# Attention scores in groups of four tiles over four PSUM banks, one PSUM bank for all transpositions, and an order of work drawn anew

## The reference

```
h = x @ W ; e = leaky_relu(h@a0 + (h@a1)^T) masked by adj ; alpha = softmax(e)
x = layernorm(x + concat(alpha @ h, h))                       # layer 0, 256 features
q, k, v = x@Wq.T+bq, x@Wk.T+bk, x@Wv.T+bv                     # layer 1, 8 heads of 64
attn = softmax(mask(q k^T / 8)) ; y = (attn @ v) @ Wo.T + bo
x = layernorm(x + y)
```

## Time and profile before

| | |
|---|---|
| time, median of 3 runs | 3236.22 us (3234.52 to 3239.79) |
| the profiled execution | 3235.14 us, of which its span is 3233.3 us |
| PE busy | 3015.4 us (93%) |
| DVE busy | 2604.6 us (81%) |
| ACT busy | 2427.2 us (75%) |
| POOL busy | 2070.5 us (64%) |
| share of the DMA engines, main queue | 73.8% |
| granted TensorE clock, mean | 0.988 |

### The profile page before, as it was taken

One profiled execution on the slowest core, in us unless ns is written; L12 is line 12 of the kernel. 1 busy time (PEld: TensorE's weight loads), 2 busy tenths in 40 slices (PEclk: granted clock), 3 DMA queues, 4 the chain that ended last, 5 costly groups with the idle time before them and its releaser, 6 DMA issues.

```text
span 3233.3 us, 60175 instructions
## 1 busy us (share of the span) xinstructions
PE 3015.4 (93%) x19084; PEld 2496.1 (77%) x19084; DVE 2604.6 (81%) x6553; ACT 2427.2 (75%) x5383; POOL 2070.5 (64%) x1799
## 2 busy tenths in 40 slices
PE   5899999999999999999999999999999999999995
PEld 4787788777787787787777787777887777887874
DVE  4888888888888888888888888888888888888873
ACT  4777777777777777877777877777877778777764
POOL 1566676666666666766666666666666666766664
PEclk8999999999999999999999999999999999999997
DMA  3777777777777777787777777777777777777774
GB/s 124 201 207 213 223 214 226 208 209 215 217 222 221 207 212 214 222 230 213 208 210 222 221 224 212 210 210 217 222 224 208 205 214 222 220 227 206 212 203 143
DMA packets 290044, 681.90 MB, mean 211 GB/s; under 512 B 40512, under 2 KB 74048, under 8 KB 256960
## 3 DMA queue, kind: packets, MB, share of 16 engines
q1 hardware_dynamic: 289728, 678.05, 73.8%
HBM read 375.40 MB, written 302.51 MB: 210 GB/s over the span
## 4 chain that ended last, share of the span: by engine, by line
PE 49%; DMA 25%; POOL 10%; SPq 5%; ACT 5%; issue 3%; DVE 3%; ACTq 0%; DVEq 0%; POOLq 0%
PE R_bank L621 30%; DMA turned_lo_prob<-scratch 17%; PE O_bank L708 9%; POOL turned_lo_prob L1054 8%; DMA scratch<-blocked 8%; PE S_bank L689 6%; SPq L523 4%; PE L_bank L612 2%; ACT turned_hi_prob L736 2%; DVE blocked L995 1%; SPq L540 1%; POOL turned L1074 1%; PE L_bank L621 1%; POOL o_pair L1049 1%; DVE prob L975 1%
## 5 line engine op out<-in xcount | busy, mean ns | idle before, releaser
L1054 POOL TENSOR_TENSOR turned_lo_prob<-turned_lo_prob,turned_hi_prob 128x512 fp32r<-128x512 f32 x1024 | 1312.0, 1312 | 671.5 <-ACT turned_hi_prob L736 671.5
L995 DVE STREAM_TRANSPOSE blocked<-prob 128x512 f32<-128x512 f32 x1024 | 695.4, 699 | 185.9 <-ACT prob L817 127.9
L736 ACT ACTIVATE turned_hi_prob<-turned_lo_prob 128x512 fp32r<-128x512 f32 x1024 | 593.5, 622 | 329.1 <-DMA turned_lo_prob<-scratch 322.8
L817 ACT ACTIVATE prob<-prob,negmax 128x512 f32<-128x512 f32 x1024 | 730.3, 714 | 89.2 <-DVE negmax L975 88.1
L975 DVE CUSTOM_DVE_ANT_0 prob<-S_bank,mask 128x512 f32<-128x512 f32 x1024 | 681.1, 679 | 83.5 <-PE S_bank L689 77.1
L689 PE MATMUL S_bank<-qk_pair 64*128 64x512 f32 x3072 | 495.3, 427 | 84.9 <-DVE negmax L975 83.5
L708 PE MATMUL O_bank<-turned_hi_prob,v_st 128*128 128x256 f32 x2048 | 517.6, 290 | 48.9 <-POOL turned_lo_prob L1054 48.5
L708 PE MATMUL O_bank<-turned_lo_prob,v_st 128*128 128x256 f32 x2048 | 508.4, 285 | 0.0
L708 PEld LDWEIGHTS O_bank<-turned_hi_prob,v_st 128*128 128x128 f32 x2048 | 396.6, 194 | 73.2 <-POOL turned_lo_prob L1054 67.9
L621 PE MATMUL R_bank<-wv,x1T 128*128 128x256 f32 x3072 | 415.4, 288 | 0.2 <-DVE v_st L874 0.2
L621 PEld LDWEIGHTS R_bank<-wv,x1T 128*128 128x128 f32 x3072 | 381.7, 191 | 38.3 <-issue 35.5
(11 more groups left out here) (75 smaller groups left out, 4315.6 us busy)
## 6 DMA issues: line engine op xcount, KB each, us to landing
scratch<-blocked SPq DMA_DIRECT2D x256, 1024.0 KB, 4.6
turned_lo_prob<-scratch SPq DMA_DIRECT2D x1024, 256.0 KB, 5.6
tokens<-xT SPq DMA_DIRECT2D x128, 256.0 KB, 5.0
tokens<-x SPq DMA_DIRECT2D x128, 256.0 KB, 4.8
r_wide<-r_scratch SPq DMA_DIRECT2D x512, 64.0 KB, 3.6
out<-tokens SPq DMA_DIRECT2D x128, 256.0 KB, 4.0
r_scratch<-r_cols SPq DMA_DIRECT2D x256, 2.0 KB
tokens<-adj SPq DMA_DIRECT2D x1, 1024.0 KB, 7.6
```

Of the source, the lines that this page charges most:

```text
L736: act.activation(dst, src, ACT.Copy).then_inc(done, 1)
L817: act.activation(prob_tile(R, s), prob_tile(R, s), ACT.Exp, bias=negmax[:, slot:slot + 1], scale=-1.0, accum_out=psum_row[:, ph % 2, j:j + ...
L995: dve.transpose(blocked[:, ph % 2, :, :, 2 * (s % 2) + s % 4 // 2, :].rearrange("p d c i -> p c d i"), prob_tile(R, s).rearrange("p (c d i ...
L1054: pool.tensor_tensor(turned_lo_prob[:, ph % 2, a, :, :], turned_lo_prob[:, ph % 2, a, :, :].bitcast(F32), turned_hi_prob[:, a, :, :].bitca ...
```

## The change

1. `scores` becomes a group of two units, four tiles, in four banks. `S_bank` has 4 banks instead of 3, tile s stands in bank s % 4, and a group waits until all four tiles of the group before it are reduced. There are 8 groups in a round where there were 16 units.
2. `L_bank` is one bank instead of two. Every solo piece waits until the one before it is taken out.
3. `N` is copied to SBUF by ACT (`n_wide`, one copy of 128x512 a round), and `pre` reads it from there. So the bank is free at once.
4. `pair` becomes `turn`: the weighted sums go to `oT` a half at a time (8 a round of 128x256 on ACT and on POOL, where there were 4 of 128x512), and the buffer `o_half` holds one half, where `o_pair` held two. `lows` of a half waits for the low part of the half before it.
5. The small buffers are packed together, and `stats` gets 2 rows instead of 4.
6. All five tables, the start, the prologue and the ending are written in a new order.

```diff
-        S_bank = [bank(f"S_bank{i}") for i in range(3)]
+        S_bank = [bank(f"S_bank{i}") for i in range(4)]
-        L_bank = [bank(f"L_bank{i}") for i in range(2)]
+        L_bank = bank("L_bank")
...
-            return S_bank[(32 * R.k + s) % 3]
+            return S_bank[s % 4]
...
-                before = solo_count(R, name, 1 - SAME_BANK.get(name, 2))
+                before = solo_count(R, name, 0)
...
-            def scores(R, u):
-                pair, t = u // T, u % T
+            def scores(R, g):
+                pair = g // 2
...
-                if t == 0:
+                if g % 2 == 0:
                     pe.wait_ge(ring_done, R.ring(f"k{pair}", 1))
-                if due(R.n(32, 2 * u - 1)):
-                    pe.wait_ge(s_red, R.n(32, 2 * u - 1))
-                for j, (qp, kp) in enumerate(PARTS):
-                    for w in range(2):
+                if due(R.n(32, 4 * g)):
+                    pe.wait_ge(s_red, R.n(32, 4 * g))
+                for u in (2 * g, 2 * g + 1):
+                    t = u % T
+                    for j, (qp, kp) in enumerate(PARTS):
+                        for w in range(2):
...
                 if kind == "pre":
                     if i == 0:
-                        act.wait_ge(n_mm, R.nx(1, 1))
+                        act.wait_ge(n_copied, R.nx(1, 1))
...
-                    act.activation(alpha[:, :], L_bank[0][:, :], ACT.Prelu, bias=terms[:, i, 0:1],
+                    act.activation(alpha[:, :], n_wide[:, :], ACT.Prelu, bias=terms[:, i, 0:1],
                                    alpha=LEAK).then_inc(a_pre, 1)
+                if kind == "N":
+                    act.wait_ge(n_mm, R.nx(1, 1))
+                    act.activation(n_wide[:, :], L_bank[:, :], ACT.Copy).then_inc(n_copied, 1)
...
-                if u % 2 == 0 and due(R.n(4, u // 2)):
-                    act.wait_ge(o_lo, R.n(4, u // 2))
+                if due(R.n(8, u)):
+                    act.wait_ge(o_lo, R.n(8, u))
...
-            def pair_hi(R, pair):
-                if pair == 0 and R.last:
+            def half_hi(R, u):
+                if u == 0 and R.last:
                     act.wait_ge(ring_mm, R.ring("O3", 1))
-                act.wait_ge(o_normed, R.n(8, 2 * pair + 2))
-                split_hi(oT[:, HI, pair % 4, :], o_pair[:, :], o_hi)
+                act.wait_ge(o_normed, R.n(8, u + 1))
+                split_hi(oT[:, HI, u // 2 % 4, o_cols(u % 2)], o_half[:, :], o_hi)
```

One line of the tables, of TensorE's near the middle of a round:

```diff
-    "E1 scores scores",
-    "V0 A3 V1",
+    "scores E1",
+    "V0 E2",
```

More of the change, by code:

```diff
@@ L77 @@
-    "B3",
+    "N k1",
+    "weigh weigh",
+    "A3 C0",
+    "scores O0",
+    "O1 O2",
+    "scores weigh",
+    "weigh O3",
+    "q2 k2",
+    "C1 D0",
+    "weigh weigh",
+    "scores D1",
+    "C2 W0",
+    "W1 W2",
+    "W3 C3",
+    "D2 weigh",
+    "weigh D3",
+    "scores q3",
+    "k3 weigh",
+    "weigh E0",
+    "scores E1",
+    "V0 E2",
+    "V1 E3",
+    "weigh weigh",
+    "B0 scores",
+    "q4 k4",
+    "weigh weigh",
+    "B1 scores",
+    "V2 V3",
+    "B2 scores",
+    "weigh weigh",
@@ L78 @@
+    "B3 q1",
 )
 SCALAR_PLAN = (
[L80 to L99 removed]
@@ L100 @@
-    "E3 exp pair exp",
-    "hi hi hi evV1",
-    "B0 hi A1 lows",
-    "exp exp evQ4 exp",
-    "lows A2 hi hi",
-    "evV2 hi exp A3",
-    "hi exp evV3 B1",
-    "exp exp B2 pair",
-    "hi hi lows B3",
-    "hi exp hi exp",
+    "N pre0 exp evQ1",
+    "aexp0 exp lows pre1",
+    "turn C0 hi hi",
+    "hi exp hi exp",
+    "exp exp exp exp",
+    "lows aexp1 hi hi",
+    "hi hi evQ2 pre2",
+    "exp C1 exp turn",
+    "aexp2 fin0 lows hi",
+    "hi pre3 hi evW0",
+    "C2 hi evW1 exp",
+    "aexp3 evW2 exp fin1",
@@ L110 @@
+    "exp evW3 C3 turn",
+    "exp hi hi hi",
+    "lows A0 fin2 hi",
+    "exp exp exp lap0",
+    "lap1 evQ3 turn exp",
+    "lap2 E0 hi hi",
+    "E1 lows hi exp",
+    "hi E2 lap3 fin3",
+    "evV0 evV1 E3 exp",
+    "exp exp turn A1",
+    "hi hi hi lows",
+    "exp exp hi B0",
+    "exp evQ4 exp turn",
+    "lows A2 hi hi",
+    "B1 hi exp exp",
+    "hi B2 evV2 evV3",
+    "A3 exp turn exp",
+    "exp lows hi hi",
+    "B3 hi turn exp",
+    "hi",
 )
 VECTOR_PLAN = (
-    "vt reduce reduce vt",
@@ L132 @@
[L132 to L143 removed]
+    "vt reduce vt reduce",
+    "red0 evQ1 vt sum",
+    "vt red1 C0 inv",
+    "reduce reduce evO0 yst0",
+    "vt reduce reduce evO1",
+    "vt vt evO2 yst1",
+    "reduce reduce vt yst2",
+    "inv vt vt evO3",
@@ new lines @@
+    "yst3 yrs reduce reduce",
+    "sum evQ2 red2 evD0",
+    "C1 vt vt reduce",
+    "inv lst0 evD1 reduce",
+    "reduce red3 evW0 lst1",
+    "evW1 sum C2 evW2",
+    "vt vt reduce evW3",
+    "evD2 C3 vt vt",
+    "lst2 evD3 lst3 inv",
+    "lrs reduce reduce reduce",
+    "sum vt vt reduce",
+    "vt evQ3 vt E0",
+    "reduce reduce reduce E1",
+    "inv sum vt E2",
+    "reduce E3 vt vt",
+    "vt inv evV0 evV1",
+    "reduce reduce reduce sum",
+    "vt vt reduce vt",
+    "B0 evQ4 vt sum",
@@ L144 @@
+    "reduce reduce reduce B1",
+    "vt reduce vt inv",
+    "reduce B2 vt vt",
+    "evV2 sum reduce evV3",
+    "inv B3",
 )
 GPSIMD_PLAN = (
-    "norm pair",
+    "norm turn",
     "lo lo",
@@ L150 @@
     "lo lo",
-    "norm yrs",
-    "norm lo",
+    "yrs norm",
+    "turn lo",
     "lo lo",
-    "lo pair",
+    "lo norm",
+    "turn lo",
+    "lo lrs",
+    "lo lo",
+    "norm turn",
+    "A0 bo0",
     "lo lo",
     "lo lo",
-    "lrs A0",
-    "norm bo0",
-    "bo1 lo",
+    "norm bo1",
+    "bo2 turn",
+    "A1 lo",
     "lo lo",
     "lo norm",
-    "pair lo",
-    "lo lo",
-    "lo A1",
-    "A2 norm",
+    "turn A2",
     "lo lo",
@@ L168 @@
     "norm A3",
-    "pair lo",
+    "turn norm",
     "lo lo",
-    "lo norm",
-    "bo2 bo3",
+    "lo lo",
+    "bo3 turn",
 )
@@ L428, in solo_bank @@
         def solo_bank(name):
-            return L_bank[name in SECOND_BANK]
+            return L_bank
         def all_rounds(eng, run):
@@ L855, in run_round @@
                             half_lows(R, i)
-                        elif kind == "pair":
-                            pair_hi(R, i)
+                        elif kind == "turn":
+                            half_hi(R, i)
                         else:
@@ L1000, in half_sum @@
                     own, _ = rows_of(w)
-                    o_ap = by_row_block(o_pair[own, o_cols(u % 2)])
+                    o_ap = by_row_block(o_half[own, :])
                     dve.wait_ge(o_lows, R.n(16, 2 * u + w + 1))
@@ L1095, in run_round @@
                             probs_lo(R, i)
-                        elif kind == "pair":
-                            pair_lo(R, i)
+                        elif kind == "turn":
+                            half_lo(R, i)
                         else:
```

189 lines of the change are left out of this document (57 added, 132 removed).

## The result

The changed kernel takes 3226.27 us (median of 9 runs, 3222.58 to 3231.2) against 3236.22 us (9 runs, 3232.68 to 3245.83): a ratio of 0.9965, 95% interval 0.9953 to 0.9977. It is faster by 0.35%, about 11 us. The forecast was 3126 us, with a range of 3065 to 3205: the direction is right, the size is a tenth of the forecast, and the time lies outside the range.

A forecast was written before the change was run, and what follows sets the result against it. TensorE, 96% busy, bounds the rounds: 97.7 us less 2.8 for groups and 0.7 for waits (4.3 to 3.6) gives 94.2, over 31 rounds 110 us less, so 3126 us; range 3065 to 3205.

The forecast's parts named there:

- A group of twelve matmuls: In scores: from first start to the next unit 1.6 us, where two lone units take 1.8 besides entry and aftermath.
- the term for the groups: Scores on TensorE: fewer changes between 128-row matmuls and 64-row pairs, 0.37 us each, save 2.8 us a round.
- Both waits for scores banks: TensorE's 1.22 us between adjacent scores units goes; 1.31 behind two `O` projections goes if VectorE is not over 1.3 late.
- that for `alpha`: TensorE's 0.82 us wait at `C0` for a first-layer exponential goes or shrinks to a few tenths.
- the bound by reductions: Rival: TensorE waits at each group for four reductions, 5 us more a round, 3275 us; chance 0.02.
- the joint that saves nothing: Rival: joining two scores units saves nothing, as weights wait for the running matmul; only waits change, 3215 us; chance 0.03.
- the walk over the four `E`: `E` transpositions through one `L_bank`: waits of 0.4 to 0.5 at `E2`, 0.8 at `E3`; with `B0` and `N` 2.0 us a round.
- E0: First of the four `E` transpositions, time zero of the walk; ScalarE has it out at 1.3 us, VectorE at 2.0.
- the rival of transfers that land 1 to 2 us later: Late probability transfers make several `weigh` wait; waits of 4.7 to 6 us a round, 3160 to 3200 us; chance 0.22.
- the packed small buffers cost nothing: In SBUF: packing the small buffers together was taken to cost no time.
- the forecast's 90.6: TensorE's busy time in us a round: the forecast round of 94.2 less 3.6 of waits.
- two lump terms: TensorE waits not placed by the walk: 1.0 us a round scattered, as now, and 0.6 because everything is 4% denser.

The follow-up runs named there:

- kernel 8: The changed kernel with the large buffers' old addresses restored and the load `mv` issued earlier on SP; 0.9761 of the kernel before, 3161.45 us.
- experiment 4: The changed kernel with a small 128-row, 2-column matmul between the two units of each scores group; 1.0091 of the kernel before, 3273.55 us.
- Experiment 5: The changed kernel with `mv` ahead of `fin2` and a `rl` ahead of `sv` in SP's list; 0.981 of the kernel before, 3181.68 us.
- kernel 3: The changed kernel with `stats0` and `psum_row` moved ahead, giving projection operands their old addresses; 0.9918 of the kernel before, 3212.75 us.
- experiments 2 and 3: Kernel before with 32 unused bytes ahead of `x1T`: 1.0034, 3255.13 us; changed kernel with projection operands at old addresses: 0.9918, 3212.75 us.
- experiment 10: The changed kernel with the twelve matmuls of `V0` done twice, into the same bank; 0.9944 of the kernel before, 3221.55 us.
- Experiment 9: Kernel 8 with the next `rs mv` ahead of the token loads `xt1 ld0` in SP's list; 0.9899 of the kernel before, 3205.32 us.

## Why the prediction was wrong

**What was right.** A group of twelve matmuls takes 1.59 us to the next unit, forecast 1.6, and breaking it costs 0.40, forecast 0.37. TensorE is busy 90.9 us a round in kernel 8, which has the addresses of before, and 93.4 in the kernel before: 2.5 less, where the term for the groups was 2.8. So the mechanism holds and the size is about right. The Trainium skill's rule (TensorEngine Tiling, Tiling Modes, Key Properties) that a change of mode drains TensorE agrees with these rows; experiment 4 gives it the price of 0.40 us for there and back. Both waits for scores banks and that for `alpha` are gone (62.1 to 4.1, 20.5 to none). The rivals of the bound by reductions and of the joint that saves nothing are refuted.

**The step that failed: the walk over the four `E`.** "ScalarE comes to `E0` behind an exponential and a `lap`", and from there on the walk let it work without a wait, which rests on the sentence that the round trip takes 4.6 + 5.6 = 10.2 us and has 11.1. The 10.2 are two medians from issue to landing. Three things were left out: the queue of SP, where `rs`, `rl` and `fin2` stand ahead of `mv` (5.10 us from store to load for 4.6), the 2.19 us for issuing its four transfers, of which the last counts, and that these transfers land in 7.1 us there and not in the median 5.6. The trace shows 14.4 us. The first `hi` waited 3.19 us, and by ScalarE's order and the one `L_bank` this became 2.76 us at `E2`, forecast 0.4 to 0.5. I had written the rival of transfers that land 1 to 2 us later, and its waits of 4.7 to 6 us a round hold the measured 5.0, but I put 0.22 on it; its time ends at 3200, since it has nothing for the busy time of the next two steps. Experiment 5 sets this step right and gives 1.4 us a round, in kernel 8 over kernel 3 1.8; its waits at `E2` and `E3` are then 0.8 and 1.3, near the walk's but still above.

**The step "the packed small buffers cost nothing".** They cost some 0.9 us of matmul time a round, 0.45 of the round, 15 us in all (experiments 2 and 3). No part of the forecast asked which addresses the operands get.

**The clock.** The forecast took the full clock of the earlier trace rows for granted. The standstill at `E2` brings it down, which adds some 0.9 us a round to TensorE's busy time (in experiment 10, without its added 1.44 us, this is 91.5 for 92.4), but by that experiment little to the time. With the 0.9 of the addresses it makes up most, if not all, of the 1.8 us by which the busy time is over the forecast's 90.6.

**The sum.** Forecast 94.2, measured 97.34, which over 31 rounds is 97 us; the two ends, for which I took nothing, add 7. Kernel 8, without the two causes, has 95.13: they make 2.2 of the 3.1 us. The other 0.9 is 0.3 of busy time (90.9 for 90.6) and 0.6 of standing (4.2 for 3.6). By place, TensorE stands there 0.7 us at `E2` and 1.2 at `E3`, where the walk had 0.4 to 0.5 and 0.8, 0.6 at `N` for 0.4, and not at all at `B0` for 0.3. Elsewhere it is 1.8 us, and the forecast had 1.6 in its two lump terms. Half of that is one wait that I had not walked: the `weigh` behind the last `k` follow it 3.77 us later instead of 2.73, since GpSimd's `lo` are late there. Experiment 9 moved their load and only exchanged the wait for another. Why `E2` and `E3` wait longer than walked, with the load on time, stays open.
